# A row tile quantised in two halves, and the first layer begun by halves of k, in a two-layer kernel on one core

## The reference, cut to what matters

```python
# layer 0: x is (8, 256, 1024), weight (1024, 1024); groups of 128 columns share a scale
lora_delta = lora_B @ lora_A * (32.0 / 64.0)
cb = codebook / max(abs(codebook))                       # 8 levels
scale = exp(scale_log)
wg = (weight + lora_delta).reshape(O, 8, 128)
normalized = wg / scale
idx = searchsorted((cb[:-1] + cb[1:]) * 0.5, normalized, side='left')
w = (cb[idx] - normalized) + normalized
w_eff = (w * scale).reshape(O, I) + lora_delta
x = x + x @ w_eff.T
# layer 1: gated MLP, W_gate, W_up (2752, 1024), W_down (1024, 2752), a rank-16 adapter per batch row on each
gate, up = lora_add(x @ W_gate.T, ...), lora_add(x @ W_up.T, ...)
out = x + lora_add((silu(gate) * up) @ W_down.T, ...)
```

## Time and profile before

| what | value |
|---|---|
| median of 3 runs | 1582.48 us (1581.64 to 1582.91) |
| the profiled execution, its own time | 1581.99 us |
| its span in the trace | 1580.3 us |
| PE busy | 1562.2 us (99%) |
| DVE busy | 1235.1 us (78%) |
| ACT busy | 565.9 us (36%) |
| granted TensorE clock, all 40 slices | 0.9 or more of full |

### The profile page before, as it was taken

One profiled execution on the slowest core, in us unless ns is written; L12 is line 12 of the kernel. 1 busy time (PEld: TensorE's weight loads), 2 busy tenths in 40 slices (PEclk: granted clock), 3 DMA queues, 4 the chain that ended last, 5 costly groups with the idle time before them and its releaser, 6 DMA issues.

```text
span 1580.3 us, 21060 instructions
## 1 busy us (share of the span) xinstructions
PE 1562.2 (99%) x6936; PEld 1284.6 (81%) x6936; DVE 1235.1 (78%) x1583; ACT 565.9 (36%) x1005; POOL 529.3 (33%) x401
## 2 busy tenths in 40 slices
PE   7999999999999999999999999999999999999999
PEld 5888888888888888877888888888888888888887
DVE  8999778878888999988777787878776576794453
ACT  6311155333333333365333333333343233233231
POOL 4410013455654556624444555555410000000000
PEclk9999999999999999999999999999999999999999
DMA  9652265677778889772445666665467667676553
GB/s 305 134 111 76 71 213 130 164 203 223 216 214 195 231 226 238 226 271 74 134 122 138 176 184 186 179 180 164 154 189 220 166 165 201 159 215 205 158 185 117
DMA packets 368460, 281.25 MB, mean 178 GB/s; under 512 B 225120, under 2 KB 266848, under 8 KB 368224
## 3 DMA queue, kind: packets, MB, share of 16 engines
q1 hardware_dynamic: 246976, 240.77, 52.3%
q10 hardware_dynamic: 119296, 33.33, 9.0%
q0 software_dynamic: 2080, 5.80, 1.8%
HBM read 166.27 MB, written 110.85 MB: 175 GB/s over the span
## 4 chain that ended last, share of the span: by engine, by line
PE 87%; DVE 9%; issue 1%; ACT 1%; ACTq 1%; DMA 1%; SPq 0%; DVEq 0%
PE bank L1884 20%; PE bankA L1884 14%; PE bankC L1884 13%; PE bank L2121 10%; PE bankC L2121 7%; PE bankA L2121 6%; PE bankT L2032 4%; PE bank L2032 4%; PE bankT L2121 3%; PE bankT L1935 1%; PE bankT L1936 1%; DVE rl L1360 1%; PE bankC L1900 1%; DVE xl L1369 1%; DVE qsum L1670 1%
## 5 line engine op out<-in xcount | busy, mean ns | idle before, releaser
L1012 ACT CAST rh<-wt 128x512 fp32r<-128x512 f32 x253 | 155.4, 620 | 378.3 <-PE bank L1884 89.3
L1360 DVE TENSOR_TENSOR rl<-wt,rh 128x512 fp32r<-128x512 f32 x253 | 243.2, 969 | 37.1 <-ACT rh L1012 36.8
L1538 DVE TENSOR_TENSOR opl<-opl,oph 128x512 fp32r<-128x512 f32 (+1 forms) x154 | 107.7, 701 | 155.4 <-ACT oph L1157 155.0
L1884 PE MATMUL bank<-xh,rh 128*128 128x512 f32 x528 | 205.8, 390 | 0.2 <-DVE rl L1360 0.2
L1884 PE MATMUL bank<-xl,rh 128*128 128x512 f32 x528 | 205.6, 389 | 0.0
L1884 PE MATMUL bank<-xh,rl 128*128 128x512 f32 x528 | 205.5, 389 | 0.0
L1157 ACT CAST oph<-opl 128x512 fp32r<-128x512 f32 (+1 forms) x154 | 95.5, 621 | 268.4 <-DMA opl<-LT_d 263.2
L1884 PE MATMUL bankC<-xh,rh 128*128 128x512 f32 x352 | 137.1, 390 | 0.0
L1884 PE MATMUL bankA<-xl,rh 128*128 128x512 f32 x352 | 137.0, 389 | 0.0
L1884 PE MATMUL bankC<-xl,rh 128*128 128x512 f32 x352 | 137.0, 389 | 0.0
L1884 PE MATMUL bankC<-xh,rl 128*128 128x512 f32 x352 | 137.0, 389 | 0.0
(11 more groups left out here) (224 smaller groups left out, 3639.2 us busy)
## 6 DMA issues: line engine op xcount, KB each, us to landing
opl<-LT_d SPq DMA_DIRECT2D x148, 256.0 KB, 2.9
WT_d<-wt SPq DMA_DIRECT2D x88, 256.0 KB, 3.3
RT_d<-dt SPq DMA_DIRECT2D x70, 256.0 KB, 3.3
opl<-RT_d SPq DMA_DIRECT2D x70, 256.0 KB, 3.8
LT_d<-ev ACTq DMA_DIRECT2D x57, 256.0 KB, 2.5
wb<-WT_d SPq DMA_DIRECT2D x44, 256.0 KB, 3.3
wt<-WT_d SPq DMA_DIRECT2D x44, 256.0 KB, 3.5
dn<-in_L_cond_W_down_dram SPq DMA_DIRECT2D x86, 128.0 KB, 3.9
```

The source lines that it names most:

```text
L1012: nc.scalar.copy(rh[:, v % RING, 0:KH * rows], wsrc(mm, RSRC[p])).then_inc(s_hi, 1)
L1360: dv.tensor_tensor(rl[:, v % RING, 0:KH * rows], wsrc(mm, RSRC[p]), rh[:, v % RING, 0:KH * rows].bitcast(f32), ALU.subtract).then_inc(s_lo, 1)
L1538: dv.tensor_tensor(opl[0:rows, L_AT[n % NL], :], opl[0:rows, L_AT[n % NL], :].bitcast(f32), oph[0:rows, L_AT[n % NL], :].bitcast(f32), ALU ...
L1884: last = te.matmul(OUT[p], a[:, u % RING, cols], b[:, OPND[p], k, :], start=k == 0 and n == 0, stop=k == KH - 1 and n == 2 and (p in (0, 1 ...
```

## The change

The chunks' units are made in another order: the first four k of chunks 0 and 1, then the last four of both, then chunks 2 and 3 (`UNITS`). The product of row tile 0 runs its first 16 steps in the same order (`STEPS`): piece 0 and piece 1 are built side by side in two banks. Row tile 0 is quantised in two halves of 512 columns, each a chain of 20 (`quantise_half`, `QH = 20`), and only 12 units stand ahead of step 0 in place of 18. The second half's transposes and `lora_delta(1)` are issued at step 4, `lb_group(2)` at step 7. The later builds move seven or eight steps back, and the tail of `ORDER` is changed. SP's loads of x are reordered, with the weight of row tile 1 loaded once the first operation of the second half is done. In layer 1's DVE list `a_lo` and `ad_lo` come before `lo(u + 3)` at some u.

```diff
+        def slot(u):
+            return u + (u >= XW) + (u >= XLB)
         def bank_of(u):
-            return bankX[(u + (u >= XFIRST)) % 4]
+            return bankX[slot(u) % 4]
...
-        XFIRST = 18
-        QS = 22
+        XFIRST, XW, XLB = 12, 18, 21
+        QS, QH = 22, 20
+        UNITS = [(c, kh * TT + k) for kh in range(2) for c in range(2) for k in range(TT)]
+        UNITS += [(c, k) for c in range(2, NC) for k in range(KD)]
+        def dq_end(o):
+            return 2 * QH + QS * o
         ORDER = [(o, c) for o in range(KD - 3) for c in range(NC)]
-        ORDER += [(KD - 3, 0), (KD - 3, 1), (KD - 3, 2), (KD - 2, 0), (KD - 2, 1), (KD - 1, 0), (KD - 1, 1)]
-        ORDER += [(KD - 2, 2), (KD - 1, 2), (KD - 3, 3), (KD - 2, 3), (KD - 1, 3)]
-        BUILD = {o: 47 + 30 * (o - 2) if o > 1 else 2 * KD for o in range(1, KD)}
+        ORDER += [(KD - 3, 0), (KD - 3, 1), (KD - 3, 2), (KD - 2, 0), (KD - 2, 1), (KD - 2, 2), (KD - 1, 0), (KD - 1, 1)]
+        ORDER += [(KD - 1, 2), (KD - 3, 3), (KD - 2, 3), (KD - 1, 3)]
+        STEPS = [(i, kh * TT + k) for kh in range(2) for i in range(2) for k in range(TT)]
+        STEPS += [(i, k) for i in range(2, KD * NC) for k in range(KD)]
+        BUILD = {o: 54 + 30 * (o - 2) if o > 1 else 3 * KD for o in range(1, KD)}
...
                     if c == NC - 1:
-                        sp.wait_ge(s_neg, KD)
+                        sp.wait_ge(s_neg, KD + TT)
...
-                load_nat(2)
+                load_nat(1)
                 load_nat(3)
                 load_nat(4)
-                sp.wait_ge(s_dq, 2)
+                load_nat(5)
+                sp.wait_ge(s_dq, QH + 1)
                 load_weight(1)
-                load_nat(5)
                 load_nat(6)
                 load_nat(7)
...
-                    if u == KD + 2:
+                    if u == 5:
                         lb_hi(1)
-                    if u == KD + 4:
+                    if u == 8:
                         act.wait_ge(s_scr, 16 * NI)
...
-                w_hi(0)
+                w_hi(0, (0,))
                 nat_hi(XFIRST)
+                for g, (i, k) in enumerate(STEPS[:KD * LAST0]):
+                    if XFIRST + g == XW - 1:
+                        w_hi(0, (1,))
+                    if XFIRST + g == XLB:
+                        lb_hi(2)
+                    if XFIRST + g < NX:
+                        nat_lo(XFIRST + g, NX)
...
+                def quantise_half(h, early, late):
+                    cols, base = slice(h * HALF, (h + 1) * HALF), QH * h
...
+                    chain(dv.scalar_tensor_tensor(out=qc[:, cols], in0=bankD(0)[h], scalar=SCALE0, in1=lw[:, cols],
+                                                  op0=ALU.mult, op1=ALU.add))
+                    after(1)
+                    chain(dv.tensor_tensor(grouped(nrm), grouped(qc), per_group(rscale), ALU.mult))
+                    after(2)
+                    chain(at_step(0))
+                    chain(at_step(1))
+                    chain(at_step(2))
+                    early()
+                    after(4)
...
-                quantise(0, lambda: None, lambda: None, lambda: None)
-                lb_lo(1)
+                quantise_half(0, lambda: None, lambda: None)
+                quantise_half(1, lambda: (lb_lo(1), w_lo(0, (0,))), lambda: None)
+                dve.wait_ge(s_dq, dq_end(0))
                 def begin_of(o):
                     if o == 1:
-                        w_lo(0)
+                        w_lo(0, (1,))
                         rest_of_scale()
...
+                    if u - 14 * NJ in (8, 10, 12, 14):
+                        a_lo(4 * (NJ - 1) + (8, 10, 12, 14).index(u - 14 * NJ))
+                    if 0 <= it - 1 < NIT and first(it - 1) and (m, p) == (0, 4):
+                        a_lo(4 * (it - 1))
+                    if m == 1 and p == 6 and 0 <= it < NIT and it % NJ != NJ - 1 and it != NJ:
+                        ad_lo(it)
                     if RING <= u + RING - 2 < 7 * NM and u % END not in (3, 3 + END // 2):
                         lo(u + RING - 2)
+                    if m == 1 and p == 5 and 0 <= it < NIT and not first(it) and it != NJ - 1:
+                        a_lo(4 * it)
...
-                        pe.wait_ge(s_dq, QS * max(1, o - 1))
+                        pe.wait_ge(s_dq, dq_end(max(0, o - 2)))
...
+                def w_groups(o, halves=(0, 1)):
+                    for kh in halves:
+                        pe.wait_ge(s_dq, dq_end(o) - 1 + kh if o > 0 else QH * (kh + 1))
...
+                    if XFIRST + g < NX:
+                        if XFIRST + g + 2 == XW:
+                            w_groups(0, (1,))
+                            lora_delta(1)
+                        if XFIRST + g + 2 == XLB:
+                            lb_group(2)
+                        if XFIRST + g + 2 < NX:
+                            nat_group(XFIRST + g + 2)
+                        nat_minus(XFIRST + g)
...
-                w_groups(0)
-                lora_delta(1)
                 nat_group(XFIRST)
                 nat_group(XFIRST + 1)
+                w_groups(0, (0,))
+                for g in range(KD * NORD):
+                    main(g)
```

196 lines of the change are left out of this document (106 added, 90 removed).

## The result

The changed kernel takes 1588.53 us (median of 6, 1586.73 to 1592.65) where the kernel before takes 1582.70. The ratio is 1.0035, with a 95% interval of 1.0024 to 1.0046: slower by 0.35%, and above the range that was given. Executions that lie far off, such as one of the kernel before at 4082 us, are left out of all ratios. The profiled execution is the fastest of the six, 1586.73 us, against 1581.99 for that of before; its span is 1585.1 us, 4.8 more.

A forecast was written before the change was run, and what follows sets the result against it. PE was taken as the bound (87% of the span). +2.8 us in layer 0, +0.6 at the hand over and -3.6 for `a_lo` and `ad_lo` gave -0.2: 1582.3 us by the median, range 1578.8 to 1586.2.

The forecast's parts named there:

- When step 0 starts: Start of layer 0's first step: at 27.9 us, 5.8 us earlier, with row tile 0 quantised in halves.
- New wait 1, at step 4: Layer 0, step 4: PE waits 2.6 us for the second half of `eff`, queued on DVE behind `w_lo`.
- PE's work after step 0 is 202.1: Layer 0, step 0 to layer 1: PE's work grows by 5.5 us to 202.1, as units and other work move there.
- New wait 2, at builds 2 and 3: Layer 0, builds of row tiles 2 and 3: PE waits for `eff`, 1.2 and 0.75 us, as q2 starts late.
- Hand over: Layer 1's first products: x's loads, sums and low parts come 5.5 us later against 5.7 of slack; 0.6 us of waits.
- `a_lo` and `ad_lo`: Layer 1's DVE list: issuing them before a low part shortens PE's waits for them, -3.6 us.
- Nothing for the end: Behind the last matmul, at the kernel's end: the forecast's sum had no term there.
- Rival D: Layer 0: the idleness at step 4 lowers PE's clock for 4.5 us, costing 2.2: 1584.5 us; chance 0.12.
- Rival A: Layer 0: halves are cheap and the wait at step 4 is 1.3 us, 3.2 us less in all: 1579.0; chance 0.14.
- Rival B: Layer 1's products 1 to 8: the hand over becomes the bound, deciding the sign from 4 us: 1586.0 or more; chance 0.13.
- C: Rival, layer 1: the new place of `a_lo` does nothing, DVE waiting for ACT's `ah` anyway; sum +3.4, 1585.7 us; chance 0.09.

The follow-up runs named there:

- set 1: First set of follow-up runs; here its rerun of the changed kernel with nothing altered: 1587.31 us, ratio 1.0027 to the kernel before.

## Why the prediction was wrong

The sum was -0.2 us against the profiled execution of before, and the profiled execution of after came out at +4.7. Step by step:

- *When step 0 starts*: 27.9 forecast, 27.85 measured. The halves, the units, the wait of DVE for ACT (1.56 shown) and q1's start (41.3 forecast, 41.28) were right.
- *New wait 1, at step 4*: 2.6 forecast, 2.40 shown, 2.57 with latency. Right.
- *"PE's work after step 0 is 202.1"* was too small. Step 0 to layer 1 took 207.35 us, less the waits 2.57 and 1.30 that is 203.5, 1.4 more. Half of it (0.7) are four gaps of 0.15 to 0.24 us ahead of units' transposes between 39 and 46 us, for which the forecast had no term. Some 0.4 were wrong in the kernel before already: its two waits at the builds are 1.05 us with their latency, not 1.4 (the second wait that the forecast gave to each build isn't in the trace), so that its work is 197.0 and not 196.6. The 0.3 that are left are work that moved and was put at 5.5 us.
- *New wait 2, at builds 2 and 3*: 1.95 forecast, nothing there. This is the step whose mechanism failed. In its place PE waited 1.3 us at step 32. The forecast had said that q2 would be late and looked only for `eff`. It missed that the low part of row tile 1 stands in the middle of that same q2. Moving `lora_delta(2)` by itself halved this wait. Here 0.65 us were forecast too much; with the 1.4 too little of the point before, layer 0 came out at +3.7 for +2.8.
- *Hand over*: 0.6 forecast, 1.57 in the trace of after, 1.34 from the new ORDER alone, and 1.0 on average of twelve traces. Mis-sized, by 0.4 on average and by 1.0 in the profiled execution: 5.7 us of slack against 5.5 was counted on the last low part of x, and the waits came a little behind it, where DVE's list (the evictions and parts of the adapter) still carried the delay.
- *`a_lo` and `ad_lo`*: -3.6 forecast. The traces give -1.9 at the same two waits every time; the medians, -2.4 in the kernel before and -2.6 in the changed one (0.9 with executions of like clock), agree with that within their intervals and with no more than that. The mechanism was right, its size was not. The forecast credited 1.0, 1.3 and 0.9 us at three waits and 0.4 at one for `ad`. The first gave 0.6, the second 1.3, the third nothing (0.70 before, 0.73 after), since the `al` that now comes first is itself the long operation; the one for `ad` went, and a new one for `al` of the same size came at 328 us, for which there was no term.
- *Nothing for the end.* 1.1 us came behind the last store. The changed kernel has 18 more operations on DVE, and a packet of instructions is fetched in its last 2 us. Adding 18 to the kernel before brought the tail (4.8), adding 24 to the changed one removed it (3.65). That the number of operations decides is shown; that the border of a block falls into DVE's last rows is the likely reason, and by which path the fetch would hold up the end is open.
- *Rival D, 0.12* was right about its mechanism. In five of the seven profiled executions with an idle time of 2.3 us or more at step 4 the granted clock fell right behind it; in none of the ten without one did it fall there, three of these with the wait filled. Between step 0 and layer 1 the price is 1.0 to 1.6 us when it happens, where 2.2 was given. It is part of why the median of after lies 1.8 us above its best execution; how large a part is not shown. A mean clock of 0.999 alone does not prove it: with 18 small operations on the kernel before four executions list it at no cost, and the profiled one has its fall in the last 4 us, when PE is done.
- Rival A had the wait at step 4 too small. Rival B had the right place and not the size (up to 1.6, not 4); its own sum is 0.5 too high too, since a wait of 3.8 in place of the 0.6 in the forecast gives 1585.5 and not 1586.0. C is refuted by the two waits that got shorter.

The Trainium skill (TensorE: Matmul & The Clock Gate, section "What's actually happening") says that an idle array falls back to the lower of two levels. By that rule the wait at step 4 costs more than its length, and the traces agree in five of seven executions: 0.72 granted from 42 to 48 us behind an artificial wait of 2.30 is one of them. In the changed kernel's first profiled execution, 1.00 was granted behind a wait of 2.40.

Summed by the traces: +3.7 in layer 0, +1.6 in the hand over, -1.6 net for the rest of layer 1, and +1.1 at the end, 4.8. In the median the clock adds to this: 0.8 us in set 1, from the executions at 1.000 alone to all of them. Of the 4.8, the 1.57 of the hand over is at the high end of what the other traces show.

No single step made the forecast wrong: it missed a wait that it looked for in another place, had three terms too favourable, and left out the end.

## What to carry to other kernels

When an operation moves later, list everything that stands behind it in its engine's order and give each piece its own due time; here the piece that hurt was a low part slipped into a quantise, not the quantise. A short wait of the bounding engine can cost half as much again through its clock, so it is better to have that engine arrive two steps later than to let it wait, if it has other work to do first. And a part of a change that gains by itself should be tried by itself: here the reorder of `a_lo` alone is 0.18% faster than the kernel before, and the rest of the change more than eats it. Last, the releaser that a profile names is the one that ended last, not always the one that was waited for: look up in the kernel what the instruction asks for.

## What was not expected of the hardware

- A packet of instructions (q14) fetched after the last store's issue goes with an end 1.1 us later: from the start of the last matmul to the end it is 4.67 to 4.80 us in all ten traces with 1601 DVE operations, 3.58 to 3.65 in the six with 1583 or 1625, and 4.0 in the one with 1607.
- Ten to sixteen more matmuls early in PE's program moved a q8 packet from 330 us to 321 to 324, and with it ACT's issue of eight loads went from 4.4 us to 5.2 to 5.5 and PE's wait from 0.36 to between 1.2 and 1.6. One kernel had the packet there and an issue of 4.5, so the link is not settled.
- Behind an idle time of 2.3 to 2.4 us the granted clock fell to the lower level in five of seven profiled executions; behind waits of 1.5 us and less it fell in none of ten.
